# Decay factors, state scaling, skips and result norm moved between engines in an mLSTM and expert block

## What is computed

```python
x = layernorm(x + mixer(x))
x = layernorm(x + experts(x))
# mixer: q, k from silu(conv(x @ W_up)), v from x @ W_up; gates ig, log_f per head
logD = where(mask, lfc_t - lfc_s, -inf) + ig_s
Dmat = exp(logD - max_s logD)
C    = (q @ k.T) / 8 * Dmat
h    = (C / (max(|sum C|, exp(-max)) + 1e-6)) @ v
out  = ((headnorm(h) * norm_w + skip * x_act) * silu(z)) @ W_down
# experts: 16 experts of width 64, top 4 by a sigmoid gate, and one shared expert
out  = sum_e combine_e * (silu(x @ win_e) * (x @ vin_e)) @ wout_e + shared(x)
```

## Time and profile before

| what | value |
|---|---|
| median of 3 runs | 883.62 us (881.48, 883.62, 888.35) |
| profiled execution, its own time | 881.61 us |
| its span | 879.9 us |
| mean granted clock of PE over the span | 0.963 |
| busy: PE, DVE | 90%, 75% of the span |
| busy: ACT, POOL | 41%, 42% of the span |

### The profile page before, as it was taken

How to read it: one execution, slowest core, us unless ns; L and a number is a source line. 1 busy time by engine, 2 the same in 40 slices (tenths; PEclk the granted TensorE clock), 3 DMA queues, 4 the chain that set the end, 5 groups by cost and what they waited for, 6 DMA issues and landing times.

```text
span 879.9 us, 17647 instructions
## 1 busy us (share of the span) xinstructions
PE 789.5 (90%) x5783; PEld 665.3 (76%) x5783; DVE 658.6 (75%) x1711; ACT 363.2 (41%) x621; POOL 372.1 (42%) x370
## 2 busy tenths in 40 slices
PE   6879967599999999999999999999999999999966
PEld 5656656488887888887878787878787878787855
DVE  5799953577777787777777777777777777778754
ACT  4757732234344344343343434343434343433231
POOL 5050018542635363636353545463535454544200
PEclk8999977689999999999999999999999999999979
DMA  4878744210404040404040404040403040400000
GB/s 119 242 244 278 272 164 129 95 49 25 131 24 131 24 131 24 131 24 131 24 131 24 132 24 131 24 131 24 131 24 131 24 131 24 131 24 25 1 12 13
DMA packets 53104, 81.01 MB, mean 92 GB/s; under 512 B 10176, under 2 KB 36952, under 8 KB 49112
## 3 DMA queue, kind: packets, MB, share of 16 engines
q1 hardware_dynamic: 53080, 80.68, 29.8%
HBM read 55.24 MB, written 25.43 MB: 92 GB/s over the span
## 4 chain that ended last, share of the span: by engine, by line
PE 38%; DVE 20%; issue 17%; DMA 11%; POOL 7%; SPq 2%; ACT 2%; POOLq 1%; DVEq 1%; ACTq 0%
DMA max_b<-max_scratch 11%; PE bank L1395 10%; PE bank L1366 5%; DVE acc L838 5%; PE bank L1370 4%; PE bank L1367 4%; PE bank L1339 3%; DVE st L990 3%; PE bank L1385 3%; DVE out_sb L1002 2%; POOL D L548 2%; POOL D L538 2%; DVE Y L1002 2%; POOL kept L567 2%; PE bank L1315 2%
## 5 line engine op out<-in xcount | busy, mean ns | idle before, releaser
L754 ACT ACTIVATE s_in<-bank 128x512 f32<-128x512 f32 x144 | 86.1, 598 | 178.5 <-PE bank L1370 177.6
L1395 PEld LDWEIGHTS bank<-ewout,h 128*128 128x128 f32 x1024 | 132.8, 191 | 8.6
L1366 PE MATMUL bank<-yT_hi,in_hi 128*128 128x512 f32 x288 | 128.8, 447 | 11.2 <-DVE h L1097 11.2
L552 POOL TENSOR_TENSOR rs<-ve,half 128x4 f32<-128x4 f32 x32 | 32.7, 1020 | 241.9 <-DVE ve L998 241.9
L1395 PE MATMUL bank<-ewout,h 128*128 128x128 f32 x1024 | 134.8, 275 | 0.0
L1097 DVE TENSOR_TENSOR h<-s_in,bank 128x512 f32<-128x512 f32 x144 | 98.1, 681 | 48.0 <-PE bank L1370 44.3
L538 POOL TENSOR_TENSOR D<-a_tok,max_b 128x512 f32<-128x512 f32 x64 | 65.5, 1044 | 120.4 <-DVE max_b L910 67.8
L1370 PE MATMUL bank<-yT_lo,in_hi 128*128 128x512 f32 x288 | 114.8, 398 | 0.0
L1367 PE MATMUL bank<-yT_hi,in_lo 128*128 128x512 f32 x288 | 114.4, 397 | 0.0
L1101 DVE TENSOR_TENSOR h<-h,bank 128x512 f32<-128x512 f32 x128 | 87.2, 681 | 14.4 <-PE bank L1385 14.4
L951 DVE TENSOR_TENSOR state<-kept,bank 64x130 f32<-64x130 f32 x128 | 36.6, 286 | 62.6 <-POOL kept L567 41.5
(11 more groups left out here) (193 smaller groups left out, 1643.7 us busy)
## 6 DMA issues: line engine op xcount, KB each, us to landing
xact_scratch<-xact SPq DMA_DIRECT2D x16, 1024.0 KB, 5.0
max_b<-max_scratch SPq DMA_DIRECT2D x15, 1024.0 KB, 7.6
xa<-xact_scratch SPq DMA_DIRECT2D x16, 512.0 KB, 6.4
silu_z<-xact_scratch SPq DMA_DIRECT2D x16, 512.0 KB, 3.7
inter_w<-inter_scratch SPq DMA_DIRECT2D x30, 256.0 KB, 7.5
x_in<-in_L_attn_x_dram SPq DMA_DIRECT2D x16, 256.0 KB, 4.8
xt_scratch<-x_t SPq DMA_DIRECT2D x16, 256.0 KB, 5.0
xT<-xt_scratch SPq DMA_DIRECT2D x16, 256.0 KB, 8.1
```

The source lines that it names most:

```text
L754: act.activation(s_in[:, j % 2], bank[4][:], ACT.Silu).then_inc(silu_done, 1)
L1366: pe.matmul(o, in_hi[:, m, j], yT_hi[:], start=True, stop=False)
L1395: i = pe.matmul(bank[7][:, k * P:(k + 1) * P], h2[:, j % 2, k * P:(k + 1) * P], w, start=(j == k == 0), stop=(j == NJ), skip_group_check=True)
```

## The change

- The state is scaled by DVE. `kept` is gone; `update_state` is now four instructions per chunk that multiply the state by its decay and add PE's update, each for one head (64 partitions, 65 columns) with a scalar per partition.
- The decay factors are made by ACT straight from max_b and the gates: 16 exponentials of 128x128 with the gate as bias. POOL masks them afterwards, filling with 0 (`masks`).
- The skip products are made by ACT in slot 1.
- On POOL, `weigh_queries` and `masks` for the next group stand behind the scaled heads and ahead of the powers rs1 and rs2.
- The statistics of z2 come after yT_low on DVE, and DVE then makes only nb2 = -mean x rs2. The result norm out_sb is four activations on ACT, in `ffn_head` of the next step, between yT_hi and ge.
- Step 1 is taken out of the loop, as no result is there to be normalised in it.

```diff
@@ groups
             mix(0, None)
-            with eng.Fori(1, NG - 1) as g:
+            mix(1, 0)
+            with eng.Fori(2, NG - 1) as g:
                 mix(g, g - 1)
@@ gpsimd
-            def args(g, kp):
...
-                    pool.tensor_tensor(
-                        D[:, kp, par],
...
-                        ALU.subtract).then_inc(arg_sub, 1)
...
+            def masks(g):
+                for q in range(4):
+                    pool.wait_ge(D_exp, nth(g, 4, q))
                     alone(pool)
-                    d = D[:, kp, par].rearrange("p k s t -> p (k s) t")
-                    pool.affine_select(out=d, in_=d, compare_op=ALU.is_ge, fill=masked, base=0,
-                                       pattern=[[0, 2 * NP], [1, P]], channel_multiplier=-1).then_inc(arg_masked, 1)
+                    d = D[:, q // 2, q % 2].rearrange("p k s t -> p (k s) t")
+                    pool.affine_select(out=d, in_=d, compare_op=ALU.is_ge, fill=zero, base=0,
+                                       pattern=[[0, 2 * NP], [1, P]], channel_multiplier=-1).then_inc(D_done, 1)
@@ gpsimd, mix
-                for k in range(NC):
...
-                    pool.tensor_tensor(kept[:], state[:], dec[:, k, :].unsqueeze(2).to_broadcast([P, NP, 2 * DV]),
-                                       ALU.mult).then_inc(kept_done[k], 1)
...
-                        pool.tensor_scalar(mixed[:, k], xa[:, k], vecs[:, k, VS:VS + 1], None, ALU.mult
-                                           ).then_inc(skip_done, 1)
-                    if k in (1, 2) and not (isinstance(g, int) and g == NG - 1):
-                        args(g + 1, k - 1)
                 for kp in range(2):
...
+                if not (isinstance(g, int) and g == NG - 1):
+                    weigh_queries(g + 1)
+                if not (isinstance(g, int) and g == NG - 1):
+                    masks(g + 1)
                 pool.wait_ge(ve1_done, g + 1)
                 power(rs1[:], ve1[:], rs1_done)
                 if f is not None:
                     ffn(f)
-                if not (isinstance(g, int) and g == NG - 1):
-                    weigh_queries(g + 1)
@@ scalar, decays
                 for q in range(4):
-                    act.wait_ge(arg_masked, nth(g, 4, q))
-                    d = D[:, q // 2, q % 2].rearrange("p k s t -> p (k s t)")
-                    act.activation(d, d, ACT.Exp).then_inc(D_done, 1)
+                    kp, par = q // 2, q % 2
+                    if q == 0:
+                        act.wait_ge(max_in, 16 * (g + 1))
+                    prev(act, C_done[kp][par], g)
+                    for k in range(2 * kp, 2 * kp + 2):
+                        for h in range(par, NH, 2):
+                            i = act.activation(D[:, kp, par, k % 2, h // 2], max_b[:, h, k * P:(k + 1) * P], ACT.Exp,
+                                               scale=-1.0, bias=a_g[:, k, h:h + 1])
+                    i.then_inc(D_exp, 1)
@@ scalar, mix
+                    if j == SKIP_SLOT:
+                        act.wait_ge(xa_in, 16 * (g + 1))
+                        prev(act, down_mm, g)
+                        for p in range(NP):
+                            act.activation(mixed[:, p], xa[:, p], ACT.Copy, scale=vecs[:, p, VS:VS + 1]
+                                           ).then_inc(skip_done, 1)
@@ scalar
+            def ffn_norm(f):
+                act.wait_ge(nb2_done, f + 1)
+                prev(act, out_stored, f, 16)
+                for k in range(NC):
+                    i = act.activation(out_sb[:, k], z2[:, k], ACT.Identity, bias=nb2[:, k:k + 1], scale=rs2[:, k:k + 1])
+                i.then_inc(out_done, 1)
@@ scalar, ffn_head
                 copy(yT_hi[:], bank[7][:]).then_inc(yT_hi_done, 1)
+                if before(f) is not None:
+                    ffn_norm(before(f))
                 act.wait_ge(logit_mm, f + 1)
@@ vector, update_state
-                dve.wait_ge(kept_done[k], g + 1)
...
-                    i = dve.tensor_tensor(state[r, :, c], kept[r, :, c], new[r, :, c], ALU.add)
+                    for s in range(NP):
+                        i = dve.scalar_tensor_tensor(state[r, s, c], state[r, s, c], now[r, s:s + 1], new[r, s, c],
+                                                     ALU.mult, ALU.add)
@@ vector, mix
                 yT_low(g)
                 if f is not None:
+                    ffn_statistics(f)
                     ffn_norm(f)
@@ vector, ffn_norm
                 dve.wait_ge(rs2_done, f + 1)
-                prev(dve, out_stored, f, 16)
-                normalise(out_sb, z2, mv2, rs2, out_done)
+                dve.scalar_tensor_tensor(nb2[:], mv2[:, :, 0], -1.0, rs2[:], ALU.mult, ALU.mult).then_inc(nb2_done, 1)
```

More of the change, by code:

```diff
@@ L153, in mixer_moe_block @@
         state = sb("state", [P, NP, 2 * DV])
-        kept = sb("kept", [P, NP, 2 * DV])
         p1 = ExitStack()
@@ L267, in mixer_moe_block @@
         rs2 = sb("rs2", [P, NC])
+        nb2 = sb("nb2", [P, NC])
         out_sb = sb("out_sb", [P, NC, E])
@@ L326, in groups, with before @@
             ffn(NG - 1)
+        def before(f):
+            return None if isinstance(f, int) and f == 0 else f - 1
         def prev(eng, s, g, per=1):
@@ L528, in _ @@
             pool.memset(vals[:, :, :, DH:DV], 1.0).then_inc(phase2_const, 1)
-            masked = pool.to_reg(NEG)
-            def args(g, kp):
-                if kp == 0:
-                    pool.wait_ge(max_in, 16 * (g + 1))
-                a_g = a_tok[:].rearrange("p b f k h -> p (b f) k h")[:, bass.ds(g, 1)].rearrange("p g k h -> p (g k) h")
-                for par in range(2):
-                    prev(pool, C_done[kp][par], g)
-                    pool.tensor_tensor(
-                        D[:, kp, par],
-                        a_g.rearrange("p k (s two) -> p two k s", two=2)[:, par, 2 * kp:2 * kp + 2]
-                        .unsqueeze(3).to_broadcast([P, 2, NP, P]),
-                        max_b[:].rearrange("p (s two) (k t) -> p two k s t", two=2, k=NC)[:, par, 2 * kp:2 * kp + 2],
-                        ALU.subtract).then_inc(arg_sub, 1)
-                for par in range(2):
-                    pool.wait_ge(arg_sub, nth(g, 4, 2 * kp + par))
+            zero = pool.to_reg(0.0)
+            def masks(g):
+                for q in range(4):
+                    pool.wait_ge(D_exp, nth(g, 4, q))
                     alone(pool)
-                    d = D[:, kp, par].rearrange("p k s t -> p (k s) t")
-                    pool.affine_select(out=d, in_=d, compare_op=ALU.is_ge, fill=masked, base=0,
-                                       pattern=[[0, 2 * NP], [1, P]], channel_multiplier=-1).then_inc(arg_masked, 1)
+                    d = D[:, q // 2, q % 2].rearrange("p k s t -> p (k s) t")
+                    pool.affine_select(out=d, in_=d, compare_op=ALU.is_ge, fill=zero, base=0,
+                                       pattern=[[0, 2 * NP], [1, P]], channel_multiplier=-1).then_inc(D_done, 1)
             def power(dst, src, s):
@@ L560, in mix @@
             def mix(g, f):
-                dec = decay[:].rearrange("p s (g k) -> p g k s", k=NC)[:, bass.ds(g, 1)].rearrange("p g k s -> p (g k) s")
-                for k in range(NC):
-                    if k:
-                        pool.wait_ge(state_done[k - 1], g + 1)
-                    else:
-                        prev(pool, state_done[NC - 1], g)
-                    pool.tensor_tensor(kept[:], state[:], dec[:, k, :].unsqueeze(2).to_broadcast([P, NP, 2 * DV]),
-                                       ALU.mult).then_inc(kept_done[k], 1)
-                    if k == 0:
-                        prev(pool, down_mm, g)
-                        alone(pool)
-                    if k < NP:
-                        pool.tensor_scalar(mixed[:, k], xa[:, k], vecs[:, k, VS:VS + 1], None, ALU.mult
-                                           ).then_inc(skip_done, 1)
-                    if k in (1, 2) and not (isinstance(g, int) and g == NG - 1):
-                        args(g + 1, k - 1)
                 for kp in range(2):
@@ L599, in _ @@
             pool.wait_ge(back_out, 1)
-            args(0, 0)
             weigh_queries(0)
-            args(0, 1)
+            masks(0)
             pool.wait_ge(back_out, BACK)
@@ L759, in ffn @@
                     ffn_slot(f, j)
+                ffn_norm(f)
             phase1_xt(0, 0)
@@ L946, in update_state @@
                 dve.wait_ge(upd_mm[k], g + 1)
-                dve.wait_ge(kept_done[k], g + 1)
+                if k:
+                    dve.wait_ge(state_done[k - 1], g + 1)
+                else:
+                    prev(dve, state_done[NC - 1], g)
+                now = decay[:].rearrange("p s (g k) -> p g k s", k=NC)[:, bass.ds(g, 1), k].rearrange("p g s -> p (g s)")
                 new = bank[0][:, 0:NP * 2 * DV].rearrange("p (s d) -> p s d", s=NP)
```

15 lines of the change are left out of this document (11 added, 4 removed).

## The result

The changed kernel takes 942.79 us (median of 4 runs, 941.53 to 943.80); beside it on the same chip the kernel before took 885.50 (median of 4, 881.48 to 888.35). The ratio is 1.0637, 95% interval 1.0592 to 1.0682. Forecast were 939 and a range of 908 to 958. The profiled execution took 942.3 for 881.6: +60.7, where the sum said +57.8.

What follows compares the result with a forecast made beforehand. PE, busy 90% of the span, was taken to bound the kernel. 14 x (3.5 - 1.0 + 1.7) = 58.8, first boundary -4 and tail +3 made +57.8 on 881.6: 939 us, range 908 to 958.

Steps and rivals of the forecast that it cites:

- The added chain: Group boundary, yT_hi to chunk 1: late statistics, power and norm before the first SiLU, plus wider update, +3.5 us each.
- The clock: PE at each of 14 boundaries: waiting close together drops the clock to half, costing 1.7 us, bounds 0 and 3.4.
- The gains: Loop boundaries: PE's waits at chunk 3 and for slot 4's h vanish, 1.0 us less each, bounds 0 to 1.0.
- The update on DVE: State update before chunk 1: four instructions at 0.25 us, 1.0 in all instead of 0.58, bounds 0.8 and 1.6.
- First boundary: Early queries leave Y undisturbed, ending PE's 1.95 us wait and the half clock behind it: -4 us, bounds 2 and 5.3.
- Hidden parts: Skips and 16 exponentials on ACT (4.8 us), masks and rs1 on POOL, later store: all in time, costing nothing.
- rival 2: Exponentials on ACT 0.39 us apart delay masks, rs1 and Y: +1.0 us per boundary, 953 us; chance 0.13.
- Tail: Last boundary: same chain, with Y and the statistics changing places in its favour, +3 us, bounds 1 and 4.
- the signs to look for: ACT waiting about 3.5 us before out_sb, PE some 2 in slot 1 and 1 to 2 before chunk 1, half clock.
- Rival 1: PE's clock stays up at the boundaries despite the new waits: 916 us; chance 0.27.
- Rival 3: Chain from yT_hi to the norm's end fits ACT's 0.85 us to spare, so faster: 865 us; chance 0.05.
- Rival 4: Boundary's shift is taken back later in the group, where PE waited for DVE anyway: within 1%; chance 0.04.

Runs made afterwards that it cites:

- e1: Changed kernel with only the norm's four ACT parts moved to slot 1 behind the skips, statistics still late: 888.77 us, 1.0020 of the kernel before.
- e2: Changed kernel with only the statistics of z2 taken ahead of Y again, norm still between yT_hi and ge: 894.93 us, 1.0075 of the kernel before.
- e3: Changed kernel with both the norm in slot 1 behind the skips and the statistics ahead of Y: 870.19 us, 0.9820 of the kernel before.
- e4: Changed kernel with eight extra unread matmuls per step on PE, in its wait ahead of slot 1's: 922.00 us, 1.0399 of the kernel before.
- e7: Kernel before with only the decay factors changed (16 exponentials on ACT, POOL masks afterwards, arguments gone from POOL): 871.77 us, ratio 0.9842.
- e10: Kernel before with only the state scaled by DVE, a one-column product standing in for POOL's: 878.79 us, ratio 0.9895.
- e6: e3 with the state scaled by POOL again ahead of DVE's update: 858.65 us, 0.9694 of the kernel before.
- e9: e8 with the state scaled by POOL again and the result's power ahead of POOL's fourth product: 844.39 us, 0.9533 of the kernel before.
- e11: Changed kernel with only the state scaled by POOL again: 934.89 us, 1.0524 of the kernel before.
- e8: Changed kernel with statistics in the next step's slot 2, power at its start, norm after slot 4's SiLU, store one step later: 856.06 us, ratio 0.9655.
- e5: Kernel before with only the result norm on ACT between yT_hi and ge, late statistics, and step 1 out of the loop: 959.08 us, ratio 1.0821.

## Why the prediction was right

**The added chain, forecast +3.5 a boundary.** Right in kind and nearly in size. Chunk 1 comes 10.34 - 6.18 = 4.16 us later after T0, less the 0.35 by which T0 is earlier: +3.81. The steps up to nb2 were within 0.1; the norm was under-sized: 1.65 us, 0.48 for each part, where I took 1.29 from the pairs of the earlier trace rows. That is the 0.3 by which the sum to chunk 1, 10.0, fell short. e1, e2 and e3 show that the order on ACT and DVE is the cause, since they undo nothing else.

**The clock, forecast +1.7.** It fell at each of the 14 boundaries, as said, and cost less: 1.0 in a regular step by e4. Half speed lasts some 6.8 us, but for most of it PE is waiting or has room; bound by PE are only the 2.96 us from chunk 1 to the next scores, 1.96 before. I had priced half-speed time as if all of it were full of work. It also covered the wait before chunk 1 that I expected to see beside it; the shift that it stood for is there. Two steps, with 10.2 us at half speed, lost 3.5 and 2.6, so that the mean over the 14 is 1.24.

**The gains, forecast -1.0.** The waits for `kept` and for h are gone. The step of the kernel before without them (310.78 to 353.60 on the transposes of Y) took 42.82, its mean over 14 steps is 44.17: the gain is 1.35. I had counted only the waits that PE shows; the shift that each leaves is larger. e7 and e10, which relieve the same wait in two ways, gain 0.73 and 0.52 a step. Together 3.81 + 1.01 - 1.35 = 3.47, where a regular step of the changed kernel (47.78) is 3.61 over 44.17; the 0.14 I can't assign.

**The update on DVE, 1.0 us.** Measured 0.96. The ledger had it as a cost on the path, +0.4 at each boundary, and it is on the path: chunk 1 starts 0.10 us behind its end in the changed kernel and in e1 to e4, and e6 and e9, with the narrow update, have chunk 1 0.4 earlier. What the ledger left out is what `kept` costs DVE's work beside it. In the kernel before that was 0.40 on the norm (e10), in e11 it is 0.41 on nb2, and in both it makes up for the width. Where `kept` falls beside nothing on the path, the width counts in full (e6, e9). The order of the parts decides its sign.

**First boundary, forecast -4.** That term held the wait of 1.95 for Y, which lies ahead of the first yT_hi, and it is gone: Y's four parts take 1.12 beside an idle POOL, and the clock is at 1.00 from the transposes on. The first step is 3.4 shorter on top. Together -5.4, just past the bound of 5.3.

**Hidden parts.** The skips cost nothing, as forecast: ACT waits 2.03 us for PE behind them. The 16 exponentials take 4.79 us, 4.8 forecast; the spacing of 0.39 on which rival 2 rested didn't occur. The last mask starts 3.20 us before the transposes of Y and rs1 ends at 461.73; PE's transposes show no wait, so rival 2 did not occur.

**Tail, forecast +3.** +6.4. There is no mixer work beside the last boundary, so PE shows the chain bare:

```profile
904.86 0.80 PE L1380 MATMUL bank<-yT_hi,in_hi 128*128 128x512 f32 x1 [4.49 <-ACT s_in L754]
```

I had taken the loop's shift, which has cover, for a place without any. The clock's part of it is 2.6 by e4.

**Not forecast.** The first yT_hi comes 4.2 us later although the wait of 1.95 for Y is gone, so 6.2 were lost ahead of it. Of these 1.5 are at group 0's first chunk, which now waits for exponentials and then masks (PE waits 3.0 us there instead of 1.7), and 2.0 in the rest of group 0: PE's waits before chunks 1 to 3 are 0.4 to 0.5 longer each (0.73, 0.48 and 0.73 before, 1.11, 0.94 and 1.11 now). The forecast had 0 for this start, with a bound of 1.5. The other 2.7 lie in the first pass, which the change doesn't touch. DVE at one place of it, beside POOL's splits of weights that had just landed:

```profile
50.28 8.24 DVE L840 SCALAR_TENSOR_TENSOR acc<-xm,vecs,acc 128x512 f32<-128x512 f32 x6
```

The six before them took 4.06. Of kernels with the same code up to the first yT_hi, e3 reaches it at 177.3, e1, e2, e4 and e8 at 180.5 to 180.7, the changed kernel at 181.6. It is chance between executions, as far as these runs tell.

**The sum.** +60.7 for +57.8 is nearer than its terms: the 14 steps made +53.5 for +58.8, the first boundary -5.4 for -4, the tail +6.4 for +3, and 6.2 were in no term. The mechanism of the loop held; that errors of both signs cancelled is luck. Of the signs to look for, ACT's wait (3.65 us before out_sb), PE's wait in slot 1 (1.95), the half clock and the longer step (3.8) came, and the wait for `kept` went; the wait of 1 to 2 us before chunk 1 did not come.

**The rivals.** Rival 1, the clock stays up at 916: the clock fell, and e4, which keeps it up, takes 922. Rival 3 asked that the norm be one that ACT need not wait for; that is e3, e6, e8 and e9, and they gain 1.8 to 4.7%. Rival 4, cancelled within 1%, asked that the shift be taken back later in the group; a regular step keeps 3.6 us of it.

## What to carry to other kernels

Ask of each instruction that is moved to an engine with time to spare what stands behind it in that queue, and what its operand still has to wait for: ACT at 46% busy cost 6% of the time because its one critical stretch was where the norm stood. Work whose result nobody needs soon goes behind the boundary, not into it, and its whole chain (statistics, power, norm) goes with it. Parts of a change must be tried apart and in their final surroundings: here one part gained in the old kernel and lost in the repaired one.

## What the runs showed of the hardware

- An activation of 128x128 with scale and bias per partition takes 0.48 us (out_sb, 64 of them), with the bias alone 0.39 (D, 256 of them). I had expected one price. The two also differ in their function.
- A DVE instruction of 128x4 with 0.16 us of its own takes 2.29 us beside a POOL product of 2.34 us (e5), and 0.57 beside one of 0.62 (e11), in 14 steps of each run.
- The fall of the clock in the loop's boundaries was averted by eight matmuls that nobody reads: e4 takes 2.2% less than the changed kernel, with the chain up to chunk 1 as long as before (T0+10.33).
- The fall did not always last as long, though the boundaries are alike (the first SiLU ends between T0+7.2 and T0+7.6): in the 14 of the changed kernel it was once 3.4 us, eleven times 6.8 and twice 10.2.
